# Deformable-convolution sampling terms taken from PSUM, column-major tokens, and a moved overflow flag in a fused conv + attention + MoE kernel

## The reference, cut to what matters

```python
x1 = gelu(layernorm(dwconv3x3(h)))
offset = x1 @ off_w + off_b                      # 8 groups x 9 points x (x, y)
m = softmax((x1 @ mask_w + mask_b).reshape(B, H, W, G, P), -1)
...
w00 = (x1 - ix) * (y1 - iy)                      # bilinear weights of the four neighbours
w01 = (ix - x0) * (y1 - iy)
...
out = (sampled * m).sum(-1)                      # sum over the 9 points
```

## Time and profile before

| | us |
|---|---|
| median of 3 runs | 101.35 |
| lowest, highest | 101.11, 101.91 |
| the profiled execution | 101.25 |
| its span | 99.6 |
| TensorE busy | 88.9 (89%) |
| VectorE busy | 60.5 (61%) |
| ScalarE busy | 48.0 (48%) |
| GpSimd busy | 24.3 (24%) |

### The profile page before, as it was taken

One profiled execution on the slowest core, in us unless ns is written; L12 is line 12 of the kernel. 1 busy time (PEld: TensorE's weight loads), 2 busy tenths in 40 slices (PEclk: granted clock), 3 DMA queues, 4 the chain that ended last, 5 costly groups with the idle time before them and its releaser, 6 DMA issues.

```text
span 99.6 us, 2868 instructions
## 1 busy us (share of the span) xinstructions
PE 88.9 (89%) x1212; PEld 59.9 (60%) x1212; DVE 60.5 (61%) x145; ACT 48.0 (48%) x106; POOL 24.3 (24%) x37
## 2 busy tenths in 40 slices
PE   4999999999897979998968798898999997799980
PEld 1455667548673959875833475474977785564330
DVE  1259863404189889999704225397830969927870
ACT  0453074469999720013002235769625889785000
POOL 7279997000000002999600000000000000500000
PEclk9999999999999999999999999999999999999999
DMA  1999100000256766500000000000000000000003
GB/s 37 364 399 349 41 0 7 0 7 0 79 143 205 208 161 193 176 13 3 7 0 7 0 0 0 7 0 0 0 0 0 0 7 0 0 0 0 0 0 109
DMA packets 3229, 6.27 MB, mean 63 GB/s; under 512 B 528, under 2 KB 1296, under 8 KB 3216
## 3 DMA queue, kind: packets, MB, share of 16 engines
q1 hardware_dynamic: 2784, 4.67, 15.2%
q10 hardware_dynamic: 432, 1.42, 3.8%
HBM read 5.16 MB, written 0.93 MB: 61 GB/s over the span
## 4 chain that ended last, share of the span: by engine, by line
PE 63%; DVE 19%; ACT 10%; issue 5%; DVEq 0%
PE ps L1130 63%; DVE terms L902 3%; DVE ym L893 2%; ACT prod L758 2%; ACT L689 1%; ACT prod L817 1%; DVE lmax L877 1%; DVE smax L968 1%; DVE lsub L880 1%; ACT prob L724 1%; DVE prod L1002 1%; DVE prod L1006 1%; DVE ln_room L918 1%; ACT samp_t L745 1%; ACT x L692 1%
## 5 line engine op out<-in xcount | busy, mean ns | idle before, releaser
L1130 PE MATMUL ps<-terms,wts 64*128 64x256 f32 (+4 forms) x104 | 17.2, 353 | 2.0 <-DVE terms L902 1.2
L1130 PEld LDWEIGHTS ps<-terms,wts 128*128 128x128 f32 (+1 forms) x104 | 13.8, 189 | 4.6 <-issue 1.7
L563 POOL TENSOR_TENSOR prod<-v_win,o_abs 128x1280 f32<-128x1280 f32 x4 | 9.6, 2427 | 22.2 <-DVE terms L902 22.2
L1130 PE MATMUL ps<-prod,ident 32*32 32x256 f32 (+1 forms) x416 | 10.6, 384 | 1.2 <-issue 1.2
L1130 PE MATMUL ps<-prod,wts 128*64 128x256 f32 (+1 forms) x56 | 10.9, 396 | 0.7 <-DVE terms L955 0.5
L638 POOL TENSOR_TENSOR terms<-terms 128x256 f32<-128x256 f32 x2 | 1.4, 728 | 35.6 <-DVE terms L1018 35.6
L1130 PEld LDWEIGHTS ps<-prod,ident 32*32 32x32 f32 (+1 forms) x416 | 6.9, 103 | 4.3 <-issue 2.5
L1130 PE MATMUL ps<-idle 128*128 128x512 bf16 x24 | 7.7, 463 | 1.3 <-DVE idle L823 1.3
L1130 PEld LDWEIGHTS ps<-prod,wts 128*64 128x64 f32 (+1 forms) x56 | 5.9, 158 | 4.5 <-ACT prod L676 1.3
L927 DVE TENSOR_TENSOR prod<-v_win,ps 128x1280 f32<-128x1280 f32 x6 | 8.5, 1468 | 0.0
L1120 DVE TENSOR_TENSOR prod<-prod,ps 128x512 f32<-128x512 f32 x8 | 5.2, 684 | 1.6 <-PE ps L1130 1.6
(11 more groups left out here) (172 smaller groups left out, 157.8 us busy)
## 6 DMA issues: line engine op xcount, KB each, us to landing
v_win<-v_padded SPq DMA_DIRECT2D x20, 128.0 KB, 2.8
wts<-in_w ACTq DMA_DIRECT2D x1, 984.0 KB, 8.2
wts<-in_w SPq DMA_DIRECT2D x1, 640.0 KB, 8.1
v_padded<-s_v SPq DMA_DIRECT2D x1, 400.0 KB, 7.8
wts<-in_w ACTq DMA_DIRECT2D x1, 280.0 KB, 4.1
x_in<-in_x SPq DMA_DIRECT2D x1, 256.0 KB, 3.2
v_padded<-v_tok SPq DMA_DIRECT2D x4, 64.0 KB, 2.0
out<-res SPq DMA_DIRECT2D x2, 128.0 KB, 1.8
```

Source lines behind the costliest of these rows:

```text
L563: g.tensor_tensor(prod[:, bl, dy, :, :].rearrange("p d (x c) -> p d x c", c=GC), win, weights.unsqueeze(3).broadcast_to([P, K5, XG, GC]), ...
L1130: return nc.tensor.matmul(out_, lhsT, rhs, start=start, stop=stop, skip_group_check=True)
```

## The change

For each `bl`:

- **Tokens.** `h_dense` and `x1` hold the pixels with the column's remainder by 4 outermost, so that `tokens()` is a run of 64 neighbours. `h_dense` is permuted by ScalarE's copy, `x1` from its origin: `sum_taps3` reads `by_tap3` with a step of 4 elements and writes `d1_ps` in a row.
- **PSUM.** Offsets x, offsets y and mask logits have a bank each: `bank(bl, 3)`, `bank(bl, 2)`, `bank(bl, 1)`. `offsets` is 24 matmuls 64x64x72 in the order y, mask, x, with a semaphore after each kind. The bias matmuls are one for each kind and stand after both `variance1`.
- **Softmax** on VectorE reads the logits from PSUM; the copy `lg` is gone.
- **Far x-terms** are one SCALAR_TENSOR_TENSOR on VectorE each: `min(o, 0) * ym` or `max(o, 0) * ym`, with `o` from PSUM. The sign of the first is made up by `minus_ident` in TensorE's sum. **Near x-terms** go to GpSimd (`near_terms`). The order of `jx` is 0, 1, 2.
- **ScalarE** makes the y-hats first, the mask's exponential fifth, and keeps a copy of the offsets for the slow path (`save_off`).
- **Flags.** TensorE sums them after `window_weights(1)`; VectorE sets `far` after the first product of `bl` = 1.
- **Windows.** `v_win` is loaded by 8 DMAs of 160 KB for each `bl`: for each half and each of the four token columns, 16 partitions with five rows each.
- `WARM["weights"]` is 3 instead of 8.

```diff
         def tokens(tile, bl, bh, xl):
-            return tile[p0:p1_, bl, xl:HW:XL]
+            return tile[p0:p1_, bl, xl * 64:xl * 64 + 64]
...
-                for dy in range(K5):
-                    for bh in range(BH):
-                        rows = bass.AP(v_dram.tensor, v_dram[BL * bh + bl, dy].offset,
-                                       [[VP * C, H], [VW, XQ], [1, VWX * C]])
-                        sp.dma_start(v_win[p0:p1_, bl, dy, :], rows).then_inc(v_windowed[bl], 16)
+                for bh in range(BH):
+                    for q_ in range(XQ):
+                        cells = bass.AP(v_dram.tensor, v_dram[BL * bh + bl, 0].offset + q_ * VW,
+                                        [[VP * C, H], [VP * C, K5], [1, VWX * C]])
+                        sp.dma_start(v_win[p0 + q_:p1_:XQ, bl, :, :], cells).then_inc(v_windowed[bl], 16)
...
+            g.tensor_scalar(minus_ident[:, :], w("ident"), -1.0, None, ALU.mult).then_inc(minus_ident_set, 1)
...
-            pool.wait_ge(terms_done, K3 * BL)
+            def near_terms(bl):
+                pool.wait_ge(ym_done, bl + 1)
+                pool.wait_ge(near_x_done, bl + 1)
+                g.tensor_tensor(terms[:, bl, 1, :, :], ym[:, bl, :, :],
+                                hat[:, bl, 1, 0, :].unsqueeze(1).broadcast_to([P, K3, NPT * XG]),
+                                ALU.mult).then_inc(near_term_done, 1)
+            near_terms(0)
+            near_terms(1)
...
-            hats(0)
-            hats(1)
+            hats_y(0)
+            mask_exp(0)
+            hats_x(0)
+            hats_y(1)
+            mask_exp(1)
+            hats_x(1)
+            over(0)
+            over(1)
...
-            def window_terms(bl, jx):
+            def far_terms(bl, jx):
                 dve.wait_ge(ym_done, bl + 1)
-                if jx != 1:
-                    dve.wait_ge(hats_done, 2 * bl + 2)
-                v.tensor_tensor(terms[:, bl, jx, :, :], ym[:, bl, :, :],
-                                hat[:, bl, jx, 0, :].unsqueeze(1).broadcast_to([P, K3, NPT * XG]),
-                                ALU.mult).then_inc(terms_done, 1)
+                dve.wait_ge(off_saved, 2 * bl + 1)
+                v.scalar_tensor_tensor(out=terms[:, bl, jx, :, :],
+                                       in0=off_ps(bl, 0).unsqueeze(1).broadcast_to([P, K3, NPT * XG]), scalar=0.0,
+                                       in1=ym[:, bl, :, :], op0=ALU.min if jx == 0 else ALU.max,
+                                       op1=ALU.mult).then_inc(terms_done, 1)
...
-                        last = mm(d1_ps(bl)[o0:o1, :], center4[:, part, :], by_tap3[:, bl, 2 * bh + part, :],
+                        last = mm(d1_ps(bl)[o0:o1, :].rearrange("p (x n) -> p x n", x=XL), center4[:, part, :],
+                                  by_tap3[:, bl, 2 * bh + part, :].rearrange("p (n x) -> p x n", x=XL),
                                   part == 0, part == 1)
...
                 for dy in range(K5 - len(POOLED)):
                     products(bl, dy)
+                    if bl and not dy:
+                        flags(0)
+                        flags(1)
...
             window_weights(0)
+            window_weights(1)
             flags(0)
             flags(1)
-            window_weights(1)
             window_sum(0)
```

More of the change, by code:

```diff
@@ L49 @@
 POOLED = (3, 4)
-WARM = {"projection": 8, "conv5": 2, "weights": 8, "close_l0": 2, "route": 4}
+WARM = {"projection": 8, "conv5": 2, "weights": 3, "close_l0": 2, "route": 4}
 QB = 4
@@ L696, in over @@
             def over(bl):
[L698 to L702, removed]
-                act.wait_ge(off_done, bl + 1)
[L704 to L717, removed]
-                    a.activation(hat[:, bl, 1, :, :].rearrange("p c n -> p (c n)"), o_abs[:, bl, :], ACT.Identity,
-                                 bias=w("one"), scale=-1.0).then_inc(near_hat[bl], 1)
-                    far_hats(0, hats_done)
-                    over(0)
-                    over(1)
@@ new lines, in over, with axis_abs, near_hat @@
+                act.wait_ge(abs_done, 2 * bl + 2)
+                a.activation(past[:, bl, :], o_abs[:, bl, :], ACT.Relu, bias=w("minus_one"),
+                             accum_out=over_sum[:, bl:bl + 1]).then_inc(over_done, 1)
+            def axis_abs(bl, axis, src):
+                a.activation(o_abs[:, bl, axis * NPT * XG:(axis + 1) * NPT * XG], src, ACT.Abs).then_inc(abs_done, 1)
+            def near_hat(bl, axis, abs_, done):
+                act.wait_ge(abs_done, abs_)
+                a.activation(hat[:, bl, 1, axis, :], o_abs[:, bl, axis * NPT * XG:(axis + 1) * NPT * XG], ACT.Identity,
+                             bias=w("one"), scale=-1.0).then_inc(done, 1)
@@ L1018, in normed3 @@
                 v.tensor_tensor(x2[:, bl, :], bank(bl, 0)[:, 0:HW], rstd3[:, bl, :], ALU.mult).then_inc(x2_done, 1)
-            for bl in range(BL):
-                softmax(bl)
-                masked_hats(bl)
-                for jx in (1, 0, 2):
-                    window_terms(bl, jx)
-            flags(0)
-            flags(1)
+            softmax(0)
+            masked_hats(0)
+            far_terms(0, 0)
+            softmax(1)
+            far_terms(0, 2)
+            masked_hats(1)
+            far_terms(1, 0)
+            far_terms(1, 2)
             for bl in range(BL):
@@ L1213, in values, with bias_rows @@
                 last.then_inc(v_done, 1)
-            def offset_bias(bl):
-                for i in range(2):
-                    mm(om_ps(bl)[:, 2 * i:2 * i + 2, 0:OM], ones[:, :],
-                       b_row[:, C:C + OM].unsqueeze(1).broadcast_to([PARTS, 2, OM]), True, False)
+            def bias_rows(bl, kinds):
+                for kind in kinds:
+                    rows = b_row[:, C + kind * NPT * G:C + (kind + 1) * NPT * G].rearrange("p (q g) -> p q g", g=G)
+                    mm(om_ps(bl, kind).rearrange("p (q x g) -> p q x g", x=XL, g=G), ones[:, :],
+                       rows.unsqueeze(2).broadcast_to([PARTS, NPT, XL, G]), True, False)
             def offsets(bl):
                 pe.wait_ge(x1_done, bl + 1)
-                for xl in range(XL):
-                    for bh in range(BH):
-                        p0, p1_ = half(bh)
-                        last = mm(om_ps(bl)[p0:p1_, xl, 0:OM], tokens(x1, bl, bh, xl), w("offmask", p0=p0, p1=p1_),
-                                  False, True)
+                for kind in (1, 2, 0):
+                    for xl in range(XL):
+                        for bh in range(BH):
+                            p0, p1_ = half(bh)
+                            into = om_ps(bl, kind).rearrange("p (q x g) -> p q x g", x=XL, g=G)[p0:p1_, :, xl, :]
+                            last = mm(into, tokens(x1, bl, bh, xl),
+                                      w("offmask", kind * NPT * G, (kind + 1) * NPT * G, p0, p1_), False, True)
+                    if kind == 1:
+                        last.then_inc(off_y_done, 1)
+                    if kind == 2:
+                        last.then_inc(mask_done, 1)
                 last.then_inc(off_done, 1)
```

88 lines of the change are left out of this document (55 added, 33 removed).

## The result

The changed kernel takes 105.19 us (median of 4, 104.66 to 107.30) against 101.33 before: a ratio of 1.037, 95% interval 1.032 to 1.043. The forecast was 101.9, its range 100.8 to 103.2. It is slower, and by more than the range allowed for.

The account below looks back on a forecast made before the run. It took one long chain of hand-overs to bound the kernel: window sums start at 42.49 (flags) + 0.26 (windows) + 0.15 (stepped read) + 0.02 = 42.92, 0.65 later, so 101.25 + 0.65 = 101.90 us, range 100.8 to 103.2.

Parts of the forecast that it names:

- the stepped read: In `sum_taps3`, reading the moving operand with a step of 4 costs 0.15, between 0 and 2.0.
- a term added to the far term: VectorE's new three-operand far term, reading PSUM, takes 0.02 longer each, bounds 0 and 0.15.
- the prediction's own signs: Profile checks: `sum_taps3` 2.0 to 2.3; wrong if window sums start before 42 or the product ahead of `far` after 41.6.
- Rival 2: In `sum_taps3`, the stepped read doubles the stage: 1.85 above the forecast, 103.7; chance 0.06.
- Layernorm, table loads and the way to the first term: Before the window weights: table loads 0.30 earlier, first window weight at 30.85 instead of 31.59, gain 0.74; logits' maximum hidden.
- The two blocks back to back: TensorE's window weights run without the hole between blocks, ending at 40.67 instead of 42.27: gain 1.60, 0.86 from the hole.
- Rival 4: Between the two window-weight blocks, the hole isn't closed: 0.86 worse, 102.8; chance 0.08.
- The flags: Ahead of the window sums, TensorE waits 1.8 us for flags set behind the first `bl` = 1 product, until 42.49.
- The windows: Window loads of `bl` = 1 land at 41.1, bounds 39.1 and 43.0, wanted at 40.84: cost 0.26.
- rival 1: Windows of `bl` = 1 land at 42.2 to 43.0, window sums start up to 1.9 later: 103.0; chance 0.17.
- Rival 3: The unexplained 0.78 hole in TensorE's window sums goes: 100.9, or 100.6 with a shorter far chain; chance 0.17.
- The rest: Window sums take their 10.8 as before, and what follows 53.05 is not touched.

Follow-up runs that it names:

- e5: The kernel before with the stepped read alone in sum_taps3, and a stepped write so that the result stays in place; 102.63 us, ratio 1.007 to the kernel before.
- e4: Changed kernel with sum_taps3 reading in a row and writing stepped, flags set ahead of the product, window loads alternating halves; 100.37 us, ratio 0.992 to the kernel before.
- e11: e8 with 8 idle matmuls instead of 3 ahead of the window weights; 102.00 us, ratio 0.974 to the kernel before.
- e8: e4 with the near y-hat of `bl` = 0 made by VectorE instead of ScalarE; 99.50 us, ratio 0.978 to the kernel before.
- e10: e4 with the near x-terms on VectorE again instead of GpSimd; 101.21 us, ratio 0.996 to the kernel before.
- e6: Changed kernel with sum_taps3 reading in a row and writing stepped, plus eight idle matmuls behind the flags; 102.17 us, ratio 1.011 to the kernel before.
- e7: e4 without the alternation of halves in the window loads; 100.44 us, ratio 0.984 to the kernel before.
- e9: e4 with the kernel before's 20 window loads of 128 KB; 100.58 us, ratio 0.988 to the kernel before.
- e12: e4 with the stepped read in sum_taps3 put back; 102.79 us, ratio 1.012 to the kernel before.

## Why the prediction was wrong, by its steps

The start of the window sums was forecast at 42.92 and came at 44.96, 2.04 later: 1.64 from the stepped read, 0.09 from the way to the first weight, -0.17 from the weights, 0.50 from the flags and windows, and -0.02 for a term added to the far term that wasn't there. Two of the prediction's own signs say so: `sum_taps3` at 3.82 for 2.0 to 2.3, and the product ahead of `far` at 43.25, where later than 41.6 was to show it wrong (1.64 of that is the stepped read again).

- **The stepped read: this step failed.** It stood in the sum at 0.15 and measured 1.79 (e1 takes it out, e5 puts it alone into the kernel before: 1.79 both). The prediction gave both ends (0 and 2.0) and chose the low one by comparing rates per column, 1.03 ns for a stepped weight load and 0.97 for the matmul. What fits here is the weight loads' ratio: 66 to 34 ns is 1.94, and the matmul went from 390 to 633 ns each while the stage went up by 1.91. The row that the prediction called nearest did say it; it was read as a speed where it was a slowdown. The Trainium skill ("SBUF — State Buffer", Door 1: The DMA port swizzle) had the rule of 16-byte lines, and the trace agrees with it now, though only one step was run, so that no run tells a line crossing from another cost of a step. Its neighbouring remark that a step in PSUM significantly slows matmuls isn't borne out here: e1 writes float32 with that step in the same 1.96 us. Rival 2 described the case, at 1.85 above the forecast for the 1.64 it came to, with a chance of 0.06.
- **Layernorm, table loads and the way to the first term: right.** 0.65 gained (11.01 to 10.36: 0.28 to the end of the second table load and 0.37 behind it); forecast 0.30 + 0.44 = 0.74. The logits' maximum and subtraction were hidden, as said.
- **The two blocks back to back: right.** From 32.73 they take 4.82 + 4.83 = 9.65, to the flags at 42.38; the forecast had 9.82, from 30.85 to 40.67. Rival 4, that the hole between them stays, fell. GpSimd's near term took 2.02, above the 1.64 worked out by size and below the bound of 2.43.
- **The flags: right in kind, and the largest loss of all.** From the end of the weights to the first window sum it takes 2.58 (42.38 to 44.96), 2.34 of it idle; the forecast had 1.82, and 0.26 for the windows, 2.08. e2 shows it: 2.03 goes with the flags moved alone.
- **The windows: right in kind, too small.** They held the product by 0.70, forecast 0.26, because four loads in a row go to one half (e3). This is rival 1's mechanism, at a part of its size: 0.44 where it allowed 1.9. (Its 103.0 goes with windows at 42.2; with 43.0 it would be 103.8.) The bytes bounded the landing, as it said, but the 205 GB/s that the forecast took for their limit was the pace of the issue: 128 KB every 0.64 us is 205 GB/s, with the DMA engines at a share of 0.65. 160 KB every 0.64 us is 256 GB/s, and e3, with halves alternating, moves 252 to 266, above the 218 of the prediction's estimate as well. (That estimate, 26.7 + 12.0 + 2.8, is 41.5 and not 41.)
- **Rival 3, the hole in the window sums that would go away: fell for the change.** The gaps are 1.25 in all, 1.20 before. They do vary: 0.35 in e4 and 0.31 in e11 without a pause ahead of the sums, 1.79 in e5, none in e1 with a pause of 3.12 and the clock down. What makes them is open.
- **The rest.** 0.16 more in the window sums, 0.16 behind them, 0.41 around the span. The first two were taken as unchanged. The profiled execution is the fastest of the four; in the others the mean clock was 0.983, 0.965 and 0.951, which the forecast had not priced.

In sum: 1.79 + 2.34 - 0.65 - 0.79 (weights without the hole, 9.89 for 10.68) + 0.16 + 0.16 is 3.0 in the span, and 0.41 around it makes the 3.4 between the two profiled executions.

## What to carry to other kernels

When a layout is changed so that one operand becomes contiguous, follow the step to where it goes: here it went into a moving operand of TensorE, where it costs 1.8 us of the stage, while in the matmul's float32 output it is free. When a stage is made faster, the flag or semaphore that used to come early becomes what the next stage waits for: place a small instruction that another engine waits for ahead of a large one that may itself have to wait. And a row of a similar case is to be carried over as a ratio as well as a rate; if the two disagree, as 0.15 and 2.0 did here, the chance belongs to both ends.

## What the runs showed of the hardware that I had not expected

- A float32 moving operand with a step of 16 bytes: 633 ns for 256 columns instead of 390, and 3.75 us for the stage instead of 1.96. A stepped write to PSUM: 390 and 1.96.
- Two equal stage times can hide a clock: the window sums took 10.93 with 5.8 us at 1.2 GHz (busy throughout) and 10.94 at 2.4 GHz (busy 9.69, gaps 1.25). A fall in the experts costs 2.9 us (49.65 for 46.7), one over the offsets 1.38 in e5 (12.39 for 11.01).
- Window loads of 160 KB, four in a row to one half of the partitions: 207 to 229 GB/s with the DMA engines full, landing 3.8. The same loads with halves alternating: 252 to 266 GB/s, landing 3.2.
- A maximum over 288 elements takes VectorE 0.46 from PSUM and took 0.66 from the copy in SBUF (L877 before, L903 after), with the same steps in both, so the copy that was dropped had made it slower, not faster.
- The time around the span is 1.65 to 1.75 in the kernel before, e5, e8, e10 and e11 and 2.03 to 2.14 in the change, e1 to e4, e6, e7, e9 and e12. Which property of a program decides between the two isn't known; it accounts for 0.4 of the loss, and for 0.3 of what e8 gains over e4.
